# Fewer zero products beside the state sums of a hybrid Mamba, expert and attention kernel, and a new entry in its plan

## The reference, cut to what matters

```python
def step(state, inp):
    h_t, d_t, g_t, B_t, C_t = inp
    dA = jnp.exp(A[None, :, :] * d_t[:, :, None])
    new = dA * state + d_t[:, :, None] * B_t[:, None, :] * h_t[:, :, None]
    y = jnp.einsum('bin,bn->bi', new, C_t) + D * h_t
    return (new, y * g_t)
```

## Time and profile before

| What | Value |
|---|---|
| three runs | 610.83, 611.22, 612.77 us, median 611.22 |
| profiled execution, own time | 610.72 us |
| its span, first to last instruction | 608.9 us |
| mean granted clock of TensorE in it | 1.000 of full speed |
| PE busy | 98% of the span |
| DVE, ACT, POOL busy | 82%, 66%, 63% |
| records of line 1097 (zero products) | 104 (52 products), between 27.8 and 110.7 us |
| records of line 1248 (sums on PE) | 64 (32 sums) |

### The profile page before, as it was taken

How to read it: one execution, slowest core, us unless ns; L and a number is a source line. 1 busy time by engine, 2 the same in 40 slices (tenths; PEclk the granted TensorE clock), 3 DMA queues, 4 the chain that set the end, 5 groups by cost and what they waited for, 6 DMA issues and landing times.

```text
span 608.9 us, 13243 instructions
## 1 busy us (share of the span) xinstructions
PE 597.1 (98%) x4612; PEld 554.9 (91%) x4612; DVE 497.1 (82%) x1079; ACT 400.2 (66%) x852; POOL 385.6 (63%) x360
## 2 busy tenths in 40 slices
PE   8999999799999999999999999999999999999997
PEld 7754886599999999999999999999999999999997
DVE  5896789788999899999999899889989895355444
ACT  7977775777687856787587858785767533526240
POOL 2495466598876987599867987698757781001000
PEclk9999999999999999999999999999999999999999
DMA  8845014121210224021222221012301000000000
GB/s 286 264 166 207 30 56 141 69 83 73 82 71 23 73 80 143 19 74 72 84 72 69 94 83 70 23 75 76 144 22 72 5 10 18 6 1 15 1 23 10
DMA packets 18467, 45.45 MB, mean 75 GB/s; under 512 B 2847, under 2 KB 13664, under 8 KB 14178
## 3 DMA queue, kind: packets, MB, share of 16 engines
q1 hardware_dynamic: 18402, 44.61, 21.1%
HBM read 40.15 MB, written 1.31 MB: 68 GB/s over the span
## 4 chain that ended last, share of the span: by engine, by line
PE 81%; DVE 2%; issue 1%; ACT 1%; DVEq 0%; ACTq 0%
PE ps L1313 26%; PE ps L1082 14%; PE ps L1083 14%; PE ps L1084 14%; PE ps L1362 2%; PE ps L1248 2%; PE ps L1279 1%; PE ps L1374 1%; PE ps L1353 1%; PE ps L1276 1%; PE ps L1077 1%; PE ps L1187 1%; PE ps L1200 1%; PE ps L1167 1%; PE ps L1097 1%
## 5 line engine op out<-in xcount | busy, mean ns | idle before, releaser
L518 POOL TENSOR_TENSOR st<-st,rows_ring 128x512 f32<-128x512 f32 x128 | 165.0, 1294 | 63.7 <-DVE st L960 63.2
L1313 PE MATMUL ps<-down,inner_ring 128*128 128x128 f32 (+1 forms) x1408 | 171.8, 274 | 0.3 <-DVE X L1045 0.3
L1313 PEld LDWEIGHTS ps<-down,inner_ring 128*128 128x128 f32 (+1 forms) x1408 | 165.7, 191 | 3.3 <-issue 1.9
L757 ACT ACTIVATE sg<-ps 128x512 f32<-128x512 f32 x176 | 104.5, 595 | 88.1 <-PE ps L1084 80.2
L960 DVE TENSOR_TENSOR_SCAN st<-dA,ps 128x512 f32<-128x512 f32 x128 | 154.8, 1212 | 2.4 <-PE ps L1248 0.7
L1031 DVE TENSOR_TENSOR inner_ring<-sg,ps 128x512 f32<-128x512 f32 x176 | 119.3, 679 | 44.5 <-ACT sg L757 20.9
L531 POOL TENSOR_TENSOR yacc<-yacc,st 128x512 f32<-128x512 f32 x96 | 123.8, 1289 | 4.1
L705 ACT ACTIVATE dA<-delta,A 128x255 f32<-128x255 f32 x256 | 104.7, 495 | 0.2
L1082 PE MATMUL ps<-xhi,up_hi 128*128 128x256 f32 x352 | 102.0, 290 | 0.0
L1083 PE MATMUL ps<-xlo,up_hi 128*128 128x256 f32 x352 | 99.5, 283 | 0.0
L1084 PE MATMUL ps<-xhi,up_lo 128*128 128x256 f32 x352 | 99.5, 283 | 0.0
(11 more groups left out here) (154 smaller groups left out, 928.5 us busy)
## 6 DMA issues: line engine op xcount, KB each, us to landing
rows_ring<-bc SPq DMA_DIRECT2D x31, 1024.0 KB, 4.7
moved_rows<-inner_ring SPq DMA_DIRECT2D x96, 32.0 KB, 1.8
inner_ring<-gate_w SPq DMA_DIRECT2D x1, 1408.0 KB, 7.8
inner_ring<-up_w SPq DMA_DIRECT2D x1, 1408.0 KB, 10.2
down<-down_w SPq DMA_DIRECT2D x2, 512.0 KB, 9.5
out<-X SPq DMA_DIRECT2D x8, 128.0 KB, 1.8
rows_ring<-bc SPq DMA_DIRECT2D x1, 768.0 KB, 5.2
X<-x SPq DMA_DIRECT2D x1, 768.0 KB, 9.0
```

The source lines that it names most:

```text
L518: nc.gpsimd.tensor_tensor(st[:, i % NST], st[:, i % NST], row, ALU.mult).then_inc(s["m_p"], 1)
L757: nc.scalar.activation(sg[:, k % 2], two(bank_of(q, 2 * j)), ACT.Silu).then_inc(s["f_sg"], 1)
L1313: ins = nc.tensor.matmul(bank_of(q, 2 * NP + e)[:, c * H:(c + 1) * H], act_in, down[0:rows, e, n, :], start=n == 0, stop=n == NB - 1)
```

## The change: what it does

```diff
-WARM = {"m_turn": 11, "m_ph": 2, "m_cv": 0, "m_xp": 5, "m_dt": 3, "turn1": 4, "ph1": 7, "cv1": 8, "early": 3, "sum":
-        2, "out": 6}
+WARM = {"m_turn": 11, "m_ph": 2, "m_cv": 0, "m_xp": 5, "m_dt": 3, "turn1": 4, "ph1": 7, "cv1": 8, "early": 1, "sum":
+        2, "sum1": 0, "out": 6}
...
-STATE = {"dbx": -2.114, "scan": -0.433, "mulC": 1.364, "sum": 4.951}
+STATE = {"dbx": -2.114, "scan": -0.433, "mulC": 1.364, "sum": 2, "sum1": 0.951}
...
                 if n > NS // 2:
-                    add_zeros(rot[0], WARM["sum"])
+                    add_zeros(rot[0], WARM["sum1" if u else "sum"])
                 elif n and u == 0:
                     add_zeros(rot[0], WARM["early"])
```

## The result

Six runs of the changed kernel took 616.0 to 618.74 us, median 618.19, against 611.03 (610.78 to 612.8) for six of the kernel before: ratio 1.0102, 95% interval 1.0085 to 1.0119. It is slower by 1%. The forecast was 613.6 and the range ended at 617.0, so the sign was right, the size too small by two thirds, and the range missed the time. The profiled execution took 616.9 us, with a span of 615.1.

A forecast was written before the change was run, and what follows sets the result against it. PE, busy 98%, was taken as the bound, with holes only before 119 us, gated by sum(0,15) and sum(1,15). Terms +0.6 + 1.6 + 0.2 = +2.4 us gave 613.1 profiled, 613.6 predicted median, range 609.6 to 617.0.

The forecast's parts named there:

- That the order changes, and which sums move,: Lag of sum from 4.951 to 2 reorders sums: sum(0,0) before m_cv(1), sum(0,9) before m_xp(1), others on PE and POOL.
- The zero products alone, 2.2 us,: Sums of sequences 0 and 1: removed products gain 1.1 us at each gate, limited by mulC(0,10) and mulC(1,15).
- Sequence 0, +0.6: Moved sum(0,0) makes PE wait 2.7 us for D * h; m_cv late, sum(0,15) at 55.4, +0.6 us.
- Sum(0,9) ahead of m_xp(1) ... I cost that at nothing: Sequence 0: small projections about 1 us late, costed at nothing because DVE scans sequence 1's decays only behind sum(0,15).
- Sequence 1, +1.6: Moved sums stall PE before sum(1,3) and sum(1,4), making sum(1,15) 1.6 us later, its gain of 1.1 included.
- The wait before sum(1,3): Sequence 1: PE reaches sum(1,3) at 73.6 and waits until 74.95, a stall of 1.3 us.
- POOL's order, +0.2: Sequences 2 to 7: sums moved earlier on POOL cost +0.2 us in all, bounds 0 and +1.5.
- It hurts what it passes: one sum, 1.3 us, ahead of the end of each next convolution: POOL, sequences 2 to 7: a moved sum delays each next convolution; tightest reader ACT's h, waiting 0.6 us without cover.
- The clock: Rival: clock falls to 1.2 GHz in sequence 1's thin stretch, about +4 on the forecast, 617.6 us; chance 0.12.
- The row at 3.28 of 5 held the clock: Argument against the clock rival: granted clock stayed 1.00 where PE was busy 3.28 of 5 us from 110 us.
- nothing: Rival: the moves cost nothing and the 2.2 us gain stays, 609.0 us; chance 0.10.
- half: Rival: stalls come but DVE catches up before scan(1,15), gates within a us of today, 611.5 us; chance 0.20.

The follow-up runs named there:

- a2: Kernel before with only the lag of sum set to 2 in all sequences, all zero products kept: 619.36 us median, ratio 1.0131.
- a1: Kernel before with only the zero products removed (one early in sequence 0, none in sequence 1), old order: 610.88 us median, ratio 0.9987.
- a4: Kernel before with one zero product instead of three before sums 1 to 8 of sequence 0, nothing else: 611.54 us median, ratio 0.9989.
- e1: Kernel before with the new lag of sum for sequence 0 alone, except sum(0,0), zero products kept: 612.62 us median of 12.
- b3: Kernel before with the new lag of sum for sequences 2 to 7 alone, so only POOL's list changes: 612.04 us median, ratio 1.0016.
- b1: Kernel before with the new lag of sum for sequence 0 alone, all zero products kept: 615.89 us median of six.
- c1: Kernel before, old order, two zero products instead of three in sequence 0 and one instead of two in sequence 1: 609.59 us median, ratio 0.9971.
- c5: c1 plus 3 and 5 plain products filling the wait in front of m_out: 609.22 us median, ratio 0.9958.
- c8: Kernel before with only plain products filling the wait in front of m_out: 611.92 us median, ratio 1.0004.

## Why the prediction was right or wrong, point by point

- **That the order changes, and which sums move,** was right, and it carries the sign: a2 loses 7.3 us at full clock by it.
- **The zero products alone, 2.2 us,** was right in both halves: by the table a1 gains 1.05 and 1.1, and in a4 sum(0,10) starts at 45.55, just behind mulC(0,10), which ends at 45.5. A product costs 0.21 to 0.22 us.
- **Sequence 0, +0.6:** measured +0.9 (56.22 less 54.81 less the late start of 0.55). The chain was right (wait, late m_cv); h came 1.95 and scan 5 2.05 us later, each less the 0.55, instead of 1.7. One step failed: "Sum(0,9) ahead of m_xp(1) ... I cost that at nothing". It named the decays as readers and missed PE itself, which waits 0.56 us for ACT between m_xp and m_dt once the sum no longer fills that time. With all zero products kept that costs 0.8 us (e1). In the changed kernel it costs little, because mulC(0,10) is late as well: it ends at 47.86 and its sum starts at 48.04, so about 0.1 of the missing 0.3 is this wait and the rest is mulC(0,10) and what stands before it.
- **Sequence 1, +1.6:** measured +2.2. The waits before sums 3 and 4 came and ended where they were worked out to end: sum(1,3) at 74.93 and sum(1,4) at 82.91 once the 1.41 us of the gate before are taken off, against 74.95 and 82.85. Scan(1,6) was 2.8 us late (88.29 less 84.08 less 1.41) against 2.6. Mis-sized: mulC(1,15) came 3.2 us late instead of 2.6 to 3.0, and sum(1,15) with it. The wait before sum(1,3) was 0.49, not 1.3: 0.4 of the difference fell on u4, which I had not looked at, and PE came there another 0.4 us later than worked out.
- **POOL's order, +0.2:** measured +0.6 in the changed kernel, +0.8 in a2 and in b3 at full clock. The step that failed is "It hurts what it passes: one sum, 1.3 us, ahead of the end of each next convolution". ACT's h did wait (0.39, 0.42 and 0.18 us), and PE shows no hole for it. But the sums also pass the norms' n_pow, which was not priced: a sum then runs on POOL while DVE makes n_ve, n_ve takes up to 1.07 us instead of 0.17, and PE waits for xlo at the first gate product.
- **The clock:** this is the step that made the range miss. It was a rival at 0.12, and all runs of the changed kernel (6 of 6) and of a1 (12 of 12) are below full clock, at 0.988 to 0.996; with the two zero products kept in sequence 1 (a4) the lowest is 0.997. It costs 2.0 us up to the second expert block (10.2 against 8.2). The rival's 4 took up to 5 us of work at half speed; here the fall ends at 124.5 us, as the dense part begins at 124.67, and much of it lies in waits (PE busy 3.29 of 5 us in 115 to 120). "The row at 3.28 of 5 held the clock" argued from one execution and one stretch. One of the three times shown of before, 612.77, lies where only runs below full clock lie (the highest of 37 at full clock is 611.60); I read it as noise. The rule of the Trainium skill cited there ("TensorE: Matmul & The Clock Gate", Part 1: The HAM clock gate, activity releases the throttle) agrees with a1: in its trace the clock went to its lower level behind a stretch with PE busy 2.61 of 5 us.
- **The sum.** 613.1 was forecast for the profiled execution and 616.9 measured. The moves made 0.9 + 2.2 + 0.6 = 3.7 instead of 2.4, the clock 2.0 and the late start 0.55. The median is another 1.3 us above the profiled execution, not the 0.5 allowed for; two of the four slowest runs had a lower mean clock (0.988 and 0.989), the other two had that of the profiled one (0.992), so part of it stays open. The rivals "nothing" and "half" are out: a2 and b1 to b3. The sign came from the moves, as argued, and not from the clock.

## What to carry to other kernels

A number in a planning table is an instruction: where one sorted list makes the order of every engine, changing a lag reorders work far from the place that was meant, and the new order must be written out and each moved wait checked against when its data is ready, and against what the moved piece used to fill. In front of a wait that comes anyway, filler work costs nothing until it is longer than the wait; cut it down to the point at which the data is just reached (here one product per late sum: the gates of c1 and a1 are 55.0 us apart alike), since cutting further gains nothing and lets PE idle. A piece that is moved into another engine's idle time can slow work elsewhere that had run undisturbed in it, as POOL's sums did DVE's n_ve. And before pricing a clock fall as unlikely from one profiled execution, look at the spread of the plain runs and at the clock of each.

## What the runs showed of the hardware that was not expected

- The kernel before ran at mean clock 1.000 in 37 of 74 runs and 0.997 in 37, the medians 1.7 us apart, with the same instructions. In the four traces with a single short fall (b3, c1, c5, c8) it begins 0.2 to 0.5 us after the first gate product of the second expert block (117.3 to 120.2 us) and lasts 3.4 us, in dense products, and the rest of the kernel is 1.5 us longer (1.6 in b3); in the 5 us ahead PE is busy 3.39 us (c8 and b3, 115 to 120 us) or 3.42 (c1, 112 to 117 us).
- With no zero products in sequence 1 every run was below full clock and the fall was longer (6.8 us in the trace of a1, 10.2 in that of the changed kernel). The fill of the wait in front of m_out did not prevent the fall (c8). Which idle time sets it off was not settled.
- The same first instructions start the states up to 0.6 us apart (sum(0,0) at 26.9 or 27.5 us). In five traces PE's first products ran at one every 0.21 us to their end instead of going over to one every 0.11: the clock came up at 7.1 to 7.6 us instead of 4.5 to 5.9.
- A DVE instruction on four numbers a partition takes 0.17 us with POOL idle and up to 1.07 us when it starts under a sum of POOL, with which it then ends (0.02 to 0.03 us behind it).
